# A residual and a product added on TensorE in the second stage of a two-layer convolution kernel

## What is computed

```python
x = x + _L0_conv_ref(_gn(x), kernel)
x = x + _L1_conv_ref(_gn(x), w_v, w1, gn_gamma, gn_beta, w2, b2)

# inside _L1_conv_ref
t = relu(group_norm(d4_1x1(x, w1), gn_gamma, gn_beta, cmid))
wgt = einsum('oi,bighw->boghw', w2, tr) + b2         # nine weights for each pixel, group of channels and symmetry
xv = d4_1x1(x, w_v)
pats = unfold_patches(xv, 3)                         # the nine shifted copies of xv
out = (wv * pats).sum(axis=4)                        # nine products, added
```

## Time and profile before

| | us |
|---|---|
| median of 3 runs | 5191.05 |
| lowest and highest | 5189.61 and 5192.18 |
| the profiled execution | 5195.25 |
| its span, first to last instruction | 5193.5 |
| VectorE busy | 4670.5 (90%) |
| GpSimd busy | 4507.4 (87%) |
| TensorE busy | 3796.5 (73%) |
| ScalarE busy | 2854.0 (55%) |
| TensorE's mean granted clock | 0.883 of full speed |

### The profile page before, as it was taken

The page is one execution under the profiler, slowest core; times in us unless marked ns, Lnnn a source line. Parts: engine busy times, 40 slices in busy tenths (PEclk is TensorE's granted clock), DMA queues, the critical chain, the costliest instruction groups (busy, mean ns, idle before and its releaser), DMA issues.

```text
span 5193.5 us, 113938 instructions
## 1 busy us (share of the span) xinstructions
PE 3796.5 (73%) x36988; PEld 1315.4 (25%) x36988; DVE 4670.5 (90%) x8017; ACT 2854.0 (55%) x4642; POOL 4507.4 (87%) x2208
## 2 busy tenths in 40 slices
PE   8999999978766767676858685767676766767642
PEld 3333333322222222222222221222222222222220
DVE  6777777736999999999999999999999999999998
ACT  7999999956444535354545454444454444535421
POOL 5888888835999999999999999999999999999999
PEclk9999999989888888898889798989898988888866
DMA  7999999943333333232324242323232333333221
GB/s 235 257 257 257 257 256 256 247 107 100 105 102 102 99 106 107 92 121 83 119 83 130 83 127 85 120 91 115 91 110 91 110 103 102 99 106 107 82 74 57
DMA packets 872814, 679.40 MB, mean 131 GB/s; under 512 B 560080, under 2 KB 822736, under 8 KB 855888
## 3 DMA queue, kind: packets, MB, share of 16 engines
q1 hardware_dynamic: 872272, 672.72, 44.2%
HBM read 404.15 MB, written 268.44 MB: 130 GB/s over the span
## 4 chain that ended last, share of the span: by engine, by line
POOL 51%; DVE 13%; issue 9%; PE 4%; POOLq 1%; ACT 1%; DMA 0%; DVEq 0%; SPq 0%; ACTq 0%
POOL acc L1027 51%; DVE prod_p L1078 3%; DVE ps L1122 2%; DVE ps L1119 2%; DVE ps L1078 1%; DVE six_t L1043 1%; DVE acc L1125 1%; DVE prod_d L1078 1%; PE ps L722 1%; PE ps L732 1%; PE ps L773 1%; DVE dev_t L1059 1%; POOLq L1024 1%; DMA xr<-x 0%; POOLq L1026 0%
## 5 line engine op out<-in xcount | busy, mean ns | idle before, releaser
L1027 POOL TENSOR_TENSOR acc<-acc,prod_p 128x1024 f32<-128x1024 f32 x1536 | 3645.0, 2373 | 267.6 <-DVE acc L1125 50.4
L1078 DVE TENSOR_TENSOR prod_p<-ps,val 128x1024 f32<-128x1024 f32 x1536 | 1852.5, 1210 | 111.2 <-POOL acc L1027 110.7
L290 PE MATMUL ps<-xn,band 64*64 64x512 f32 x8192 | 949.2, 599 | 22.1 <-issue 13.7
L773 PE MATMUL ps<-t,w 128*32 128x256 f32 x9216 | 614.0, 425 | 435.7 <-ACT t L936 225.5
L760 PE MATMUL ps<-xm,base 128*32 128x256 f32 (+1 forms) x8192 | 636.2, 445 | 166.4 <-ACT val L923 73.7
L732 PE MATMUL ps<-xh,wh 128*32 128x512 f32 x6144 | 706.8, 600 | 49.6 <-ACT val L923 33.7
L1078 DVE TENSOR_TENSOR prod_d<-ps,val 128x512 f32<-128x512 f32 x1024 | 693.1, 677 | 25.7 <-ACT ps L929 24.0
L722 PE MATMUL ps<-xr,base 128*32 128x512 f32 x4096 | 547.1, 659 | 213.3 <-ACT val L923 124.1
L923 ACT ACTIVATE val<-ps 128x512 f32<-128x512 f32 (+1 forms) x640 | 339.8, 555 | 619.5 <-DVE prod_p L1078 418.0
L322 POOL TENSOR_TENSOR x_out<-x_out,x_in 128x512 f32<-128x512 f32 x512 | 636.2, 1275 | 0.0
L250 ACT ACTIVATE x_out<-ps 64x512 f32<-64x512 f32 x1024 | 606.1, 592 | 52.1 <-PE ps L290 31.8
(11 more groups left out here) (73 smaller groups left out, 3180.1 us busy)
## 6 DMA issues: line engine op xcount, KB each, us to landing
x_in<-x SPq DMA_DIRECT2D x128, 1024.0 KB, 7.4
x<-x_out SPq DMA_DIRECT2D x256, 512.0 KB, 5.2
xr<-x SPq DMA_DIRECT2D x512, 256.0 KB, 3.5
acc<-x SPq DMA_DIRECT2D x1024, 128.0 KB, 2.9
out<-acc SPq DMA_DIRECT2D x256, 512.0 KB, 2.7
prod_p<-wsrc SPq DMA_DIRECT2D x1, 384.0 KB, 4.6
w<-w2t SPq DMA_DIRECT2D x1, 288.0 KB, 4.6
shift_m<-shifts SPq DMA_DIRECT2D x1, 256.0 KB, 5.5
```

The lines of the kernel that those rows point to most:

```text
L290: mm = nc.tensor.matmul(ps[to:to + H2, 2 * two + t, :], band[rows, v, rows], group(xn[rows, k % N_RING, :], XP, W, v, 2 * two + x), start= ...
L773: mm = nc.tensor.matmul(taps_of(tap)[32 * q:32 * q + 32, :], w2[:, kt, tap * 32:(tap + 1) * 32], t[:, kt, u, q * UPX:(q + 1) * UPX], start ...
L1027: nc.gpsimd.tensor_tensor(acc[:, r, :], acc[:, r, :], prod_p[:, k % P_RING, :], ALU.add).then_inc(p_added, 1)
L1078: return nc.vector.tensor_tensor(dst.rearrange("p (m r w) -> p m r w", m=count, w=W), taps_of(tap).rearrange("p (m r w) -> p m r w", m=1, ...
```

## The change

In each half VectorE now makes the products of taps 0 (into bank 7), 1, 2 and 3. When products 0 and 1 are there, TensorE adds the residual and product 1 onto bank 7 with two matmuls by an identity (`add_two`). VectorE waits for them, then adds products 2 and 3. The large products are those of taps 4 to 8, five a granule, and GpSimd adds five. The late ones are j = 3 and 4.

Because TensorE now has work that is due in each half, its order is written anew: in granule n first `add_two` of half 0, then late taps, inverse and forward, then values, then `add_two` of half 1, then block transforms and early taps. `lead` is gone; its parts stand in granules 14 and 15. Some chunks stand in other granules, and ScalarE and the semaphore counts follow. The small statistics tiles share memory with `x1_bias`, the identity is loaded with the other matrices, and the group norm's epsilon and affine steps have no large product between them.

```diff
-D_TAPS, P_TAPS = (0, 1, 2), (3, 4, 5, 6, 7, 8)
+D_TAPS, P_TAPS = (0, 1, 2, 3), (4, 5, 6, 7, 8)
-P_LATE = (4, 5)
+P_LATE = (3, 4)
-FORWARD_AT = {0: 0, 1: 1, 2: 2, 4: 3, 6: 4, 7: 5, 8: 6, 9: 7}
+FORWARD_AT = {0: 0, 1: 1, 2: 2, 5: 3, 6: 4, 7: 5, 9: 6, 10: 7}
+INVERSE_AT = {2: (0,), 3: (1,), 5: (2,), 6: (3,), 9: (4,), 10: (5,), 11: (6, 7)}
 BLOCK_V_AT = {1: 0, 2: 1, 4: 2, 5: 3, 8: 4, 9: 5, 12: 6, 13: 7}
 BLOCK_T_AT = {1: (0,), 2: (1,), 4: (2,), 5: (3,), 8: (4,), 9: (5,), 10: (6, 7)}
-INVERSE_AT = {1: (0,), 2: (1,), 4: (2,), 5: (3,), 8: (4,), 9: (5,), 11: (6, 7)}
...
+        def add_two(i, n, half):
+
+            pe.wait_ge(own, i * (OWN * N_GRAN) + OWN * n + OWN // 2 * half + 2)
+            if half == 0:
+                pe.wait_ge(resid_in[n % ACC_RING], i * (64 * N_GRAN // ACC_RING) + 64 * (n // ACC_RING + 1))
+            nc.tensor.matmul(ps[:, D_BANK, :], same, acc[:, n % ACC_RING, half * HALF:(half + 1) * HALF],
+                             start=False, stop=False, skip_group_check=True)
+            nc.tensor.matmul(ps[:, D_BANK, :], same, prod_d[:, 0, :], start=False, stop=True, skip_group_check=True)\
+                .then_inc(pe_added, 1)
...
-        def period(i, more=True):
+        def period(i, more=True, begin=False):
             Ring.base, Ring.n = i * PERIOD_MM, LEAD_MM
             for n in range(N_GRAN):
-                if n > 0 and n % GRANS == 0:
-                    tap_weights(i, n // GRANS, LATE)
+                u = n // GRANS
+                add_two(i, n, 0)
+                if n % GRANS == 0 and not (begin and n == 0):
+                    tap_weights(i, u, LATE)
+                if more:
+                    for c in INVERSE_AT.get(n, ()):
+                        inverse(i + 1, c)
+                    if n in FORWARD_AT:
+                        forward(i + 1, FORWARD_AT[n])
+                    if n == MOMENTS_AT:
+                        means(i + 1)
+                        pe.wait_ge(xm_edges, EDGES * (i + 2))
+                        values(0)
+                        variances(i + 1)
+                    if n == N_GRAN - 1:
+                        values(1)
                 if n + AHEAD < N_GRAN:
                     values(n + AHEAD)
+                add_two(i, n, 1)
                 if more:
                     if n in BLOCK_V_AT:
                         block_v(i + 1, BLOCK_V_AT[n])
                     for c in BLOCK_T_AT.get(n, ()):
                         block_t(i + 1, c)
-                    if n in FORWARD_AT:
-                        forward(i + 1, FORWARD_AT[n])
-                    for c in INVERSE_AT.get(n, ()):
-                        inverse(i + 1, c)
+                    if n == N_GRAN - 1:
+                        values(2)
+                        tap_weights(i + 1, 0, EARLY)
                 if n % GRANS == GRANS - 1 and n < N_GRAN - 1:
-                    tap_weights(i, n // GRANS + 1, EARLY)
-            if more:
-                lead(i + 1)
+                    tap_weights(i, u + 1, EARLY)
...
+                    if n == N_GRAN - 1:
+                        relu(i + 1, 0)
+                        keep_values(i + 1, 1)
+                if n == 0:
+                    relu(i, 3)
                 if n + AHEAD < N_GRAN:
                     keep_values(i, n + AHEAD)
-                if n == 0:
-                    relu(i, 3)
...
+                    if n == N_GRAN - 1:
+                        keep_values(i + 1, 2)
+                        relu(i + 1, 1)
+                        tap_bias(i + 1, 0, EARLY)
+                        relu(i + 1, 2)
...
-        def opening(i, n, a, between):
+        def half_sum(i, n, a, between):
...
             if not fresh:
-                dve.wait_ge(own, g - 1)
-            product(n, 1, prod_d[:, 0, :], m0, QM // 2).then_inc(own, 1)
-            if not fresh:
                 dve.wait_ge(own, g)
             product(n, 0, ps[:, D_BANK, :], m0, QM // 2).then_inc(own, 1)
+            product(n, 1, prod_d[:, 0, :], m0, QM // 2).then_inc(own, 1)
+            between(0)
             if a == 0:
                 tap_wait(i, n, 1)
             product(n, 2, prod_d[:, 1, :], m0, QM // 2).then_inc(own, 1)
-            if a == 0:
-                dve.wait_ge(resid_in[r], i * (64 * N_GRAN // ACC_RING) + 64 * (n // ACC_RING + 1))
-            dve.wait_ge(own, g + 2)
-            nc.vector.tensor_tensor(ps[:, D_BANK, :], ps[:, D_BANK, :], acc[:, r, half], ALU.add).then_inc(own, 1)
-            between(0)
-            dve.wait_ge(own, g + 4)
-            nc.vector.tensor_tensor(ps[:, D_BANK, :], ps[:, D_BANK, :], prod_d[:, 0, :], ALU.add).then_inc(own, 1)
             between(1)
+            product(n, 3, prod_d[:, 2, :], m0, QM // 2).then_inc(own, 1)
+            dve.wait_ge(own, g + 3)
+            dve.wait_ge(pe_added, i * (2 * N_GRAN) + 2 * n + a + 1)
+            nc.vector.tensor_tensor(ps[:, D_BANK, :], ps[:, D_BANK, :], prod_d[:, 1, :], ALU.add).then_inc(own, 1)
             dve.wait_ge(own, g + 5)
-            nc.vector.tensor_tensor(acc[:, r, half], ps[:, D_BANK, :], prod_d[:, 1, :], ALU.add).then_inc(own, 1)
+            nc.vector.tensor_tensor(acc[:, r, half], ps[:, D_BANK, :], prod_d[:, 2, :], ALU.add).then_inc(own, 1)
```

## The result

The changed kernel takes **5352.96 us** (median of 4 runs, 5345.43 to 5353.58), against 5191.55 for the kernel before in the same series. The ratio is 1.031, with a 95% interval from 1.029 to 1.033: 161 us slower. The forecast was 5170 with a range of 4990 to 5290, so the prediction was wrong, in its sign too. The span of the profiled execution is 5351.6 us.

A forecast was written before the change was run, and what follows sets the result against it. GpSimd's additions were taken to set the pace at 247.9 us an image; afterwards VectorE's 227.9, waits 19.6 and clock 1.0 made 248.5. 15 images at +0.6 (+9) and the last at -31 gave 5170 us, range 4990 to 5290.

The forecast's parts named there:

- the clock: TensorE's slow clock while it rests, longest about granules 13 to 15, was counted at 1.0 us per image.
- the last image's gain: The last image prepares no next one: 28.8 us from 16 granules plus 2.5 from GpSimd's shorter tail, -31.
- GpSimd unloaded: GpSimd makes five additions per granule, 12.58 us instead of 15.10, 201 per image, and ceases to be the bound.
- The ring's 0.4: A product into the ring waits for GpSimd's addition three places back: 0.4 us per image.
- VectorE's own time: VectorE's work per image without waits: granules 205.5, statistics and affine part 16.0, dependent starts 5.1 us.
- The dependency's price: A VectorE instruction directly behind the one it depends on starts 0.12 us later, three places a granule.
- The forecast's 5.1: Total per image, in us, for VectorE instructions directly behind their predecessors, at 0.12 a place, three places a granule.
- Granule 0: VectorE waits for TensorE's pair behind late product, tap, forward transform, ScalarE's copy, relus and values: 4.9 us per image.
- Granules 1 to 15: VectorE's waits for TensorE's pair where work is bunched, in granules 2, 3, 5, 6, 9 and 10: 10.9 us per image.
- the lateness that costs nothing: TensorE's pair may come 1.5 us late in a half before VectorE has to wait.
- Tap bias: Behind granule 15's values, copy and relus, VectorE waits for ScalarE's tap bias before granule 0's product: 3.6 us per image.
- The slower one (5260): Rival: TensorE becomes the bound because its clock falls inside the image; three falls cost 6 us an image; chance 0.31.

The follow-up runs named there:

- Experiment 5: The changed kernel with VectorE making product 1 before product 0 in each half; 5340.41 us, ratio 1.029.
- Experiment 3: The changed kernel with two images in each pass of TensorE's loop, so it turns back 7 times instead of 14; 5327.68 us, ratio 1.025.
- experiment 2: The changed kernel with ScalarE's two relus of unit 3 moved from granule 0 to the end of granule 6; 5302.79 us, ratio 1.021.
- experiment 6: The changed kernel's arithmetic with TensorE's and ScalarE's order rewritten and TensorE's loop turning between granules 14 and 15; 5004.86 us, ratio 0.964.
- experiment 7: The rescheduled kernel (TensorE's and ScalarE's order rewritten) with TensorE's loop turning at the image's end again; 5016.25 us, ratio 0.967.
- the last experiment: The rescheduled kernel with product 1 first, epsilon's instruction two products earlier and VectorE's loop turning once in two images; 4929.34 us, ratio 0.949.

## Why the prediction was wrong

The mechanism was the right one: VectorE freed from GpSimd, then held by TensorE where its work is bunched, and by the tap bias at the image's end. Two steps failed: TensorE's work in granule 0 left out the turn of its loop, and the clock was put at 1.0 us per image where it cost about 3.4. The sum was 11 us per image too low, 15 times, and the last image's gain 15 too high.

**GpSimd unloaded: right.** Its additions fell by a sixth; it now waits for VectorE. The ring's 0.4 was nothing in the changed kernel.

**VectorE's own time: 2.7 too low.** The dependency's price was right: an independent small product starts 0.60 us behind the one before it, the second add and the product behind it 0.73 (2696.58, 2697.31, 2698.04 in the crowded granule above), so 0.13 each. Experiment 5 frees one of a granule's three such places and gave back 13 us, of 16 x 16 x 0.13 = 33 at most. The forecast's 5.1 itself doesn't follow from its words: three places in each of 16 granules at 0.12 are 5.8. Statistics stand between in five granules, which leaves 43 places; at 0.13 they come to 5.6. The Trainium skill, "VectorE: DVE Perf Modes", section "The DRAIN you can't avoid", has it, from a measurement on copies, that a semaphore between two operations costs nothing extra; these starts of products and adds don't agree. Half of the 2.7 is the affine part: the earlier trace rows gave it 3.35, with 0.94 for its first instruction, and now

```profile
2758.92 2.29 DVE L1081 TENSOR_TENSOR x_bias<-x_bias,gam 128x2 f32<-128x2 f32 x1 [0.82 <-POOL x_bias L1025]
2761.25 0.16 DVE L1083 TENSOR_TENSOR x_bias<-x_bias,ps 128x2 f32<-128x2 f32 x1
2761.44 2.25 DVE L1085 TENSOR_TENSOR x_bias<-bet,x_bias 128x2 f32<-128x2 f32 x1
2763.61 0.69 DVE L1089 TENSOR_TENSOR ps<-ps,val 128x512 f32<-128x512 f32 x1
```

it takes 4.69 from 2758.92 to 2763.61. Most of the other half belongs to the waits: where VectorE waits for the pair it also loses the 0.08 us by which its add would have overlapped the product in front of it. From that product's start to the add's, less the idle time, is 0.645 us in the mean of all 32 halves instead of 0.60, which is 1.4 us per image.

**Granule 0: the first failed step, 4.9 against 8.2.** I added up TensorE's instructions and left out the turn of its loop. It stood in the trace of before, in a row that I had not read:

```profile
2714.93 1.49 PE L760 MATMUL ps<-xm,base 128*32 128x384 f32 x14 [3.14 <-issue]
```

There no pair for VectorE stood behind it. The change put a matmul directly behind the turn for which VectorE waits. Experiment 3 prices the turn at about 3 us per image. Without it, in image 1 and in every second image of experiment 3, granule 0 waits 5.4, so the rest of the sum was 0.5 too low. The turn makes 2.4 of the mean 8.2, and in images 4 to 6 the clock fell within granule 0, which makes the remaining 0.3. The relus, which I had in it, are worth 3.6 with what follows from them (experiment 2).

**Granules 1 to 15: the second failed step, 10.9 against 16.0.** The crowded granules were nearly right: 3, 5, 6, 9 and 10 had 8.4 and gave 9.6. So was the lateness that costs nothing. The sum gives 1.36 us (4.66 - 1.28 - 2.02), I took 1.5, and the trace has 1.4: in granule 5's first half the pair starts 1.5 late and VectorE waits 0.1. The term that was mis-sized is TensorE's clock. I counted 1.0 us per image, because the pairs would keep TensorE from long rests. But TensorE rests 2.84 us in front of granules 1 and 7, and up to 9.7 us at a time in 13 to 15, and its clock fell behind these rests. At the lower level the stretch behind the pair of granule 1 takes 9.6 us instead of 7.9. Against image 4, where the clock stayed up and VectorE waited nothing in granule 1 and 0.5 in the first half of granule 2, that is 1.0 us per image in granule 1 and 0.6 in granule 2. Granule 7 has the same work and waits 1.0. Granules 13 to 15, where the slow pairs take up to 3.8 us and VectorE leaves them 3.4, wait 0.9. Together the clock cost about 3.4 there, an estimate from these rows, since no run holds the clock fixed. With 0.4 left over in granule 2 and 1.2 in the crowded ones that is the 5.1 that were missing.

**Tap bias: 3.6 against 5.2.** Right in granule 0 (3.8). The taps of unit 2, in front of granule 8, cost 1.4, which I had let go by with "little to wait since the tap's bias follows".

**The last image: 31 against 16.** It was 238.7 us before, not 16 x 15.10, and is 222.7 now. It isn't the 213 of granules of 13.3, since VectorE waits in it too: 5.1 us for pairs, 3.7 for the tap bias, 1.3 for the ring, 0.6 for itself.

**The rivals.** The slower one (5260) was the nearest, and only in part for its reason. It had TensorE's clock fall inside the image, at its pauses, and that did happen, in granules 1, 7 and 13 to 15, but for 3.4 us of an image and not 6; the larger part of the loss is the turn, the crowded stretches, the tap bias and VectorE's own time. The mean of the granted clock rose all the same, from 0.87 to 0.94 between 2000 and 4600 us. It missed the 0.95 that I had named and stayed above 0.9, and so the mean hid the falls that mattered. Nor did the total load decide, as experiment 6 shows. I priced the error of the forecast case at 3 us per image, 45 in all. It was 11 per image: the waits are what is left over from sums of 5 to 8 us per stretch, so a few tenths missing in each stand in full in the result, and an item that was not counted at all (the turn) belongs to no such error.

## What to carry to other kernels

Work that an engine does far ahead may be bunched; once a second engine waits for it several times in a round, its order counts more than its sum. Here the same instructions took 5353 us or 5005. Before such a link is added, lay the work of each stretch between two waits beside the other engine's time for that stretch, including the turn of the loop and the level of the clock behind each rest, and place the turn where nobody waits. When one wait is removed, look what stood behind it: VectorE's own turn, hidden before, was next with 3 us per image.

## What the runs showed of the hardware

**A loop's turn costs its engine some 3 us** in which it waits for nothing that the profile shows: 2.3 to 2.8 on TensorE in the changed kernel, 2.7 to 3.5 on VectorE. It is paid only where that engine is the late one: about 3 us per image in experiment 3, 0.8 (11 us in 14 turns) in experiment 7. In the changed kernel TensorE's clock stayed up behind 12 of its 13 turns in front of images 2 to 14 (pair 1.9 us); behind one, in front of image 6, the pair took 3.6.

**A short rest in front of a pair can double the pair's time.** Behind 2.84 us without work, in front of granule 1's pair, the clock went to its lower level, 0.50 (1.2 of 2.4 GHz), in 13 images of 14 and stayed at its upper level in one, and the pair took 3.2 to 3.7 us against 1.9. In experiment 2 the same rest was followed by the upper level in 12 images of 14. So the length of the rest alone did not decide.

**A tiny VectorE instruction with both inputs in SBUF can take as long as an addition of GpSimd.** L1081 reads 0.16 us in the first image's preparation, when GpSimd does not add, and 2.29 afterwards. The timeline of GpSimd in the kernel after, beside the rows of L1081 and L1085 above:

```profile
2758.86 9.83 POOL L1038 TENSOR_TENSOR acc<-acc,prod_p 128x1024 f32<-128x1024 f32 x4
```

GpSimd starts an addition at 2758.86, 0.06 ahead of L1081, and one addition takes 2.37 us: L1081 ends at 2761.21, when that addition ends. The second addition starts 2.49 behind the first, at 2761.35, and L1085, from 2761.44 to 2763.69, lasts until that one ends. L1083 falls between the two additions and takes 0.16. An instruction that meets an addition halfway waits for the rest of it, unless one of its inputs is in PSUM. Half a granule earlier GpSimd makes five additions in a row, 2.51 us apart, the fourth of them from 2748.29 to 2750.67:

```profile
2740.76 12.41 POOL L1038 TENSOR_TENSOR acc<-acc,prod_p 128x1024 f32<-128x1024 f32 x5 [1.40 <-DVE acc L1132]
...
2749.54 0.15 DVE L1068 TENSOR_TENSOR x_bias<-x_bias,ps 128x2 f32<-128x2 f32 x1
2749.72 0.97 DVE L1070 TENSOR_TENSOR x_bias<-x_bias 128x2 f32<-128x2 f32 x1
```

L1068 reads PSUM with one input and takes 0.15 in the middle of that addition. L1070, with both inputs in SBUF, starts 1.43 into it and ends at 2750.69. This is also why the affine part grew with the change: its first instruction started 1.43 us into an addition before (0.94 long), and stands directly behind the root now, where GpSimd has just begun one.

In the last experiment the first instruction of the affine part runs ahead of GpSimd's next addition (GpSimd starts at 2599.46, L1086 at 2599.16) and takes 0.15:

```profile
2599.16 0.15 DVE L1086 TENSOR_TENSOR x_bias<-x_bias,gam 128x2 f32<-128x2 f32 x1
2599.34 0.16 DVE L1088 TENSOR_TENSOR x_bias<-x_bias,ps 128x2 f32<-128x2 f32 x1
2599.53 2.30 DVE L1090 TENSOR_TENSOR x_bias<-bet,x_bias 128x2 f32<-128x2 f32 x1
...
2599.46 7.36 POOL L1043 TENSOR_TENSOR acc<-acc,prod_p 128x1024 f32<-128x1024 f32 x3 [3.33 <-DVE acc L1137]
```

The third instruction, again with two inputs in SBUF, comes 0.07 behind GpSimd's start and takes 2.30. The Trainium skill, "GPSIMD Engine Reference", section "1. Specifications", says that GpSimd shares its SBUF interfaces with VectorE and names VectorE's instructions with two SBUF inputs among those that contend. These rows agree, and show the size: what is left of GpSimd's instruction, up to the whole of it. An experiment that removes GpSimd's addition alone was not made.
